# A new head for a diffusion-plus-convolution kernel: negated coefficients, adding DMAs, both divergences on TensorE, another order on every engine

## The reference, cut to what matters

```
s  = groupnorm(x)                                   # 32 groups of 2 channels
g  = relu(bn(dwconv3x3(s, wg)));   g1 = relu(bn(dwconv3x3(s, wg1)))
gy, gx = sobel(s)
Bx = 0.2 / (gy*gy/4 + 1);          By = 0.2 / (gx*gx/4 + 1)
E  = 0.2 * 0.5 * (roll(g,1,W) - roll(g,-1,W) + roll(g1,1,C) - roll(g1,-1,C))   # the divergence
D  = 1 / (1 + 2Bx + 2By);          c0 = 1 - 2Bx - 2By
for 5 steps:                                        # h starts as s, h0 as s
    h, h0 = D*(c0*h0 - 2E*h + (-Ax+2Bx)*roll(h,1,W) + (Ax+2Bx)*roll(h,-1,W)
                 + (-Ay+2By)*roll(h,1,C) + (Ay+2By)*roll(h,-1,C)) + 0.4*D*s,  h
x  = x + relu(bn(h));   x = x + relu(conv3x3(groupnorm(x), ternary(W)) + b)
```

## Time and profile before

| what | us |
|---|---|
| median of 3 runs | 327.84 |
| the profiled execution | 327.07 |
| its span | 324.1 |
| VectorE busy | 270.0 (83%) |
| TensorE busy | 254.3 (78%) |
| ScalarE busy | 129.1 (40%) |
| GpSimd busy | 7.2 (2%) |

### The profile page before, as it was taken

How to read it: one execution, slowest core, us unless ns; L and a number is a source line. 1 busy time by engine, 2 the same in 40 slices (tenths; PEclk the granted TensorE clock), 3 DMA queues, 4 the chain that set the end, 5 groups by cost and what they waited for, 6 DMA issues and landing times.

```text
span 324.1 us, 5181 instructions
## 1 busy us (share of the span) xinstructions
PE 254.3 (78%) x2252; PEld 228.0 (70%) x2252; DVE 270.0 (83%) x224; ACT 129.1 (40%) x198; POOL 7.2 (2%) x25
## 2 busy tenths in 40 slices
PE   0125779999887999997008999999999987788794
PEld 0114569797776996686008999998998977776683
DVE  1896343499899999579999999999999999997921
ACT  3235569905671252512002244152351150451943
POOL 1000000000000000001000001011010000000000
PEclk9999986557995589999656999999999999799999
DMA  7540000000000000000600003361951003000033
GB/s 255 167 157 0 0 0 5 1 2 2 0 2 2 2 2 0 0 2 0 129 0 2 0 2 65 67 129 18 231 111 35 1 0 131 0 2 0 0 129 129
DMA packets 5173, 14.44 MB, mean 45 GB/s; under 512 B 2336, under 2 KB 2336, under 8 KB 4128
## 3 DMA queue, kind: packets, MB, share of 16 engines
q0 software_dynamic: 720, 5.24, 8.0%
q1 hardware_dynamic: 4144, 8.16, 7.7%
q10 hardware_dynamic: 288, 0.72, 0.7%
HBM read 6.79 MB, written 2.10 MB: 27 GB/s over the span
## 4 chain that ended last, share of the span: by engine, by line
DVE 34%; PE 12%; issue 3%; ACT 1%; DVEq 0%; ACTq 0%
DVE ring L796 21%; PE psum L1048 5%; PE psum L1121 4%; DVE first_two L872 3%; DVE stats L809 2%; PE psum L956 2%; DVE coef L839 2%; DVE coef L804 1%; DVE coef L755 1%; DVE coef L771 1%; DVE first_two L576 1%; DVE coef L850 1%; ACT coef L325 0%; DVE lo L845 0%; DVE mv L812 0%
## 5 line engine op out<-in xcount | busy, mean ns | idle before, releaser
L796 DVE TENSOR_TENSOR ring<-coef,state 128x2048 f32<-128x2048 f32 x51 | 113.5, 2290 | 6.2 <-ACT state L325 5.1
L1048 PE MATMUL psum<-mats,ring 128*128 128x128 f32 x816 | 96.0, 277 | 7.0 <-DVE ring L796 6.9
L1048 PEld LDWEIGHTS psum<-mats,ring 128*128 128x128 f32 x816 | 90.9, 143 | 10.6 <-DVE ring L796 10.2
L325 ACT ACTIVATE state<-psum 128x1024 f32<-128x1024 f32 x36 | 35.1, 1024 | 94.2 <-PE psum L1048 60.0
L1007 PEld LDWEIGHTS psum<-coef,state 32*128 32x128 f32 x768 | 36.1, 289 | 2.0 <-issue 2.0
L1007 PE MATMUL psum<-coef,state 32*128 32x64 f32 x768 | 36.8, 378 | 0.0
L1048 PE MATMUL psum<-mats,first_two 128*128 128x128 f32 x144 | 20.7, 306 | 18.6 <-DVE first_two L576 18.6
L576 DVE SCALAR_TENSOR_TENSOR coef<-coef 128x2048 f32<-128x2048 f32 x15 | 34.4, 2291 | 0.4
L1048 PEld LDWEIGHTS psum<-mats,first_two 128*128 128x128 f32 x144 | 19.0, 161 | 18.9 <-issue 18.8
L325 ACT ACTIVATE coef<-psum 128x512 f32<-128x512 f32 (+1 forms) x22 | 17.2, 792 | 33.6 <-PE psum L1007 21.4
L985 PE MATMUL psum<-hi_s,sobel_m 128*128 128x512 f32 (+2 forms) x48 | 21.1, 443 | 7.0 <-DVE lo_s L638 5.8
(11 more groups left out here) (123 smaller groups left out, 265.1 us busy)
## 6 DMA issues: line engine op xcount, KB each, us to landing
first_two<-coef POOLq DMA_DIRECT2D x5, 1024.0 KB, 7.1
coef<-in_x SPq DMA_DIRECT2D x2, 1024.0 KB, 5.8
coef<-in_wide_taps SPq DMA_DIRECT2D x4, 384.0 KB, 4.2
ring<-in_x SPq DMA_DIRECT2D x2, 512.0 KB, 6.4
ring<-in_x SPq DMA_DIRECT2D x1, 1024.0 KB, 9.0
out<-coef SPq DMA_DIRECT2D x2, 512.0 KB, 3.1
out<-coef SPq DMA_DIRECT2D x4, 256.0 KB, 2.5
mats<-in_matrices ACTq DMA_DIRECT2D x1, 384.0 KB, 6.1
```

The costliest lines, as they stand in the source:

```text
L325: return nc.scalar.activation(dst, src, func, **kw)
L796: V.tensor_tensor(wc(ring[:, slot, :]), wc(coef[:, t, a, :]), h_at(t, k, dw, dc), ALU.mult)\
L1048: ins = mm(slot_ap(name)[:, (j % 8) * 128:(j % 8) * 128 + 128], src[:, j * 128:j * 128 + 128], ident, is_transpose=True, start=first and j ...
```

## The change

All of it is in the head. The steps keep their products, in another order.

1. The coefficients are made negated (ScalarE negates when it takes a sum out, `keep_turned`), which lets one scalar-tensor-tensor do what took two operations. `over_rows` and `over_channels` are two operations each and make `AXP` and 2gD in `AXM` (`AYP`, `AYM` likewise); a DMA issued by GpSimd then adds `AXP` to `AXM`. `scaled_g`, `plus_columns`, `minus_columns` and one operation of `over_channels` are gone.
2. Tile 0's divergence goes to TensorE too (`dv_0_0`, `dv_0_1`); both tiles' divergences stand ahead of the first step.
3. The reordered copy is made on VectorE from the centred tile and the inverse root (`scale_grouped`) rather than by ScalarE from the scaled one. `split_hi(1)` moves from ScalarE to VectorE, `shifted` of tile 0 stays there.
4. Centring, squaring and summing the squares go by halves.
5. The taps lie in planes 6 and 5 of tile 1 and in a buffer of their own, so planes 3 and 4 are free; their transfers are issued before and just behind the second tile's `x`. The ternary weights lie in ring buffer 2.
6. In the Sobel jobs all the matmuls on the high part come first. The order of the jobs, of their slots and of the work on every engine is another one.
7. All the second tile's diffusivities come before step (0,0), and its remaining coefficients between steps (0,0) and (1,0) rather than behind (1,0).

```diff
-A0, AE, FS, AXM, AXP, AYM, AYP = 1, 3, 0, 6, 4, 2, 5
+A0, AE, FS, AXM, AXP, AYM, AYP = 1, 6, 0, 3, 4, 2, 5
...
-        taps_m = coef[:, 1, 3:5, :].rearrange("p a n -> p (a n)")[:, 0:CG * 6 * W]\
-            .rearrange("p (g y v n) -> p g y v n", g=CG, y=3, v=2)
+        taps_at = [coef[:, 1, 6, 18 * C:18 * C + 4 * 6 * W], coef[:, 1, 5, 0:10 * 6 * W], last_taps[:, :]]
...
-        wtern = coef[:, 1, 6, 18 * C:27 * C]
+        wtern = ring[:, 2, 0:9 * C]
...                                                    # GpSimd, ahead of its other DMAs
+            for t in range(TILES):
+                pool.wait_ge(axp_ready, t + 1)
+                pool.dma_start(coef[:, t, AXM, :], coef[:, t, AXP, :], accum_op=ALU.add).then_inc(ax_full[t], 16)
+                pool.wait_ge(ayp_ready, t + 1)
+                pool.dma_start(coef[:, t, AYM, :], coef[:, t, AYP, :], accum_op=ALU.add).then_inc(ay_full[t], 16)
...                                                    # ScalarE
-                frees(copy(turned(t, k + 1, h), slot_ap(name)), name)
+                frees(copy(turned(t, k + 1, h), slot_ap(name), scale=-1.0), name)
...                                                    # VectorE
+            def scale_grouped(t):
+                dve.wait_ge(xm_ready, 2 * t + 2)
+                rs = gsum[:, t, 3, :].rearrange("p (a g) -> p a g", a=CP).unsqueeze(3).unsqueeze(4)
+                V.tensor_tensor(s_grouped[t].rearrange("p (g e a w) -> p a g e w", e=2, a=CP, w=W),
+                                h_at(t, 0).rearrange("p w (a g e) -> p a g e w", a=CP, e=2),
+                                rs.broadcast_to([128, CP, CG // 2, 2, W]), ALU.mult).then_inc(s_grouped_ready, 1)
...
+            def over_rows(t):
+                taken_out(t)
+                dve.wait_ge(d_ready, 2 * t + 1)
+                then(stt(coef[:, t, AXM, :], gN[t], 2.0, coef[:, t, 0, :], ALU.mult, ALU.mult))
+                stt(coef[:, t, AXP, :], coef[:, t, AXM, :], -0.5, coef[:, t, AXP, :], ALU.mult, ALU.add)\
+                    .then_inc(axp_ready, 1)
...
-                for i, (a, dw, dc) in enumerate(((AYM, 0, -1), (AYP, 0, 1), (AXM, -1, 0), (AXP, 1, 0), (AE, 0, 0))):
+                for i, (a, dw, dc) in enumerate(((AYP, 0, 1), (AXP, 1, 0), (AE, 0, 0), (AXM, -1, 0), (AYM, 0, -1))):
...
             denominator(0)
-            ternary()
             split_lo(1)
             newton(0)
-            diffusivities(0)
...                                                    # TensorE
+            to_depthwise(0, 0)
+            to_depthwise(0, 1)
+            pe.wait_ge(sobel_m_ready, 4)
+            for g in range(2):
+                for h in range(2):
+                    sobel(0, g, h)
+            group_var(1)
+            depthwise(0, 0)
+            depthwise(0, 1)
...
+            depthwise(1, 0)
+            divergence(0, 0)
+            divergence(0, 1)
+            depthwise(1, 1)
+            divergence(1, 0)
+            divergence(1, 1)
```

More of the change, by code:

```diff
@@ L334, in square_of @@
             def square_of(t):
-                act.wait_ge(xm_ready, t + 1)
-                copy(wc(square), h_at(t, 0), ACT.Square).then_inc(sq_ready, 1)
+                if t:
+                    act.wait_ge(vsum_ready, 2)
+                for h in range(2):
+                    act.wait_ge(xm_ready, 2 * t + h + 1)
+                    copy(wc(half(square, h)), h_at(t, 0, w0=h * W // 2, w1=(h + 1) * W // 2), ACT.Square)\
+                        .then_inc(sq_ready, 1)
             def wrap(t, k, done):
@@ L524, in _ @@
                 keep_turned(k, t, 1)
-                if (k, t) == ORDER[0]:
-                    d_of(1)
                 keep_state(k, t, 0)
@@ L677, in ternary @@
                 wait_reader(dve, "wsum")
-                then(V.tensor_scalar(wred[:, 2:3], wred[:, 1:2], -1.0, None, ALU.mult))
+                V.tensor_scalar(wred[:, 2:3], wred[:, 1:2], -1.0, None, ALU.mult)
+            threshold()
+            scale_s(0)
+            split_hi(0)
+            split_lo(0)
+            centre(1)
+            sum_squares(1)
+            def ternary():
+                dve.wait_ge(vsum_ready, 4)
                 then(V.tensor_scalar(wtern, wabs, wred[:, 1:2], None, ALU.is_gt))
@@ L684, in ternary, with shifted @@
                 signal(stt(wtern, wl, wred[:, 1:2], wabs, ALU.is_ge, ALU.subtract), tern_ready, 1)
+            def shifted(t):
+                for h in range(2):
+                    wait_reader(dve, f"gx_{t}_{h}")
+                V.tensor_scalar(coef[:, t, 2, :], coef[:, t, 1, :], (1.0 + 2 * DT) * S, None, ALU.add)\
+                    .then_inc(shifted_ready, 1)
             def denominator(t):
@@ L709, in newton @@
-                then(stt(c[3], c[3], -2.0, y_first[t], ALU.add, ALU.mult))
-            def diffusivities(t):
-                c = [coef[:, t, i, :] for i in range(NCOEF)]
-                then(stt(c[4], c[1], S, c[3], ALU.add, ALU.mult))
-                then(stt(c[5], c[0], S, c[3], ALU.add, ALU.mult))
-                signal(V.tensor_tensor(c[2], c[4], c[5], ALU.add), sb_ready, t + 1)
-            def divergence(t):
+                then(stt(coef[:, t, 5, :], coef[:, t, 0, :], S, coef[:, t, 3, :], ALU.add, ALU.mult))
@@ L741, in divergence_taken, with source @@
+            def source(t):
                 for h in range(2):
                     wait_reader(dve, f"dv_{t}_{h}")
[L744 to L751 removed]
@@ L866, in step @@
                     dve.wait_ge(halo_ready, 4 * states_through(k - 1, t))
-                for i, (a, dw, dc) in enumerate(((AYM, 0, -1), (AYP, 0, 1), (AXM, -1, 0), (AXP, 1, 0), (AE, 0, 0))):
+                for i, (a, dw, dc) in enumerate(((AYP, 0, 1), (AXP, 1, 0), (AE, 0, 0), (AXM, -1, 0), (AYM, 0, -1))):
+                    if k == 0 and i == 0:
+                        dve.wait_ge(ayp_ready, t + 1)
+                        dve.wait_ge(axp_ready, t + 1)
+                        for h in range(2):
+                            wait_reader(dve, f"dv_{t}_{h}")
+                    if k == 0 and a == AXM:
+                        dve.wait_ge(ax_full[t], 16)
+                    if k == 0 and a == AYM:
+                        dve.wait_ge(ay_full[t], 16)
                     multiply(t, k, a, dw, dc)
@@ L873, in step @@
                         .then_inc(kept_made[t], 1)
+            ternary()
+            ask_scale(1)
+            shifted(0)
+            rsqrt(128, GROUPS, gsum[:, 1, 3, :])
             denominator(0)
-            ternary()
+            scale_grouped(1)
+            scale_s(1)
+            split_hi(1)
             split_lo(1)
             newton(0)
-            diffusivities(0)
+            across_columns(0)
+            across_rows(0)
+            both_diffusivities(0)
             wait_job(dve, "alpha")
@@ L1153, in _ @@
             small("wsum", 1, ones[:, :], wred[:, 0:1])
+            to_depthwise(0, 0)
+            to_depthwise(0, 1)
+            pe.wait_ge(sobel_m_ready, 4)
+            for g in range(2):
+                for h in range(2):
+                    sobel(0, g, h)
+            group_var(1)
+            depthwise(0, 0)
             depthwise(0, 1)
-            pe.wait_ge(kept_ready, 1)
-            small("alpha", 2, ones[:, :], wred[:, 3:5])
+            to_depthwise(1, 0)
+            to_depthwise(1, 1)
             for g in range(2):
@@ L1159, in _ @@
                     sobel(1, g, h)
-            to_depthwise(1, 0)
-            to_depthwise(1, 1)
+            pe.wait_ge(kept_ready, 1)
+            small("alpha", 2, ones[:, :], wred[:, 3:5])
             depthwise(1, 0)
+            divergence(0, 0)
+            divergence(0, 1)
             depthwise(1, 1)
+            divergence(1, 0)
+            divergence(1, 1)
             last = None
             for k, t in ORDER:
-                if last == ORDER[0]:
-                    divergence(1, 0)
-                    back_to_natural(*last)
-                    divergence(1, 1)
-                    add_source(t, k)
-                elif last and last[0] < STEPS - 1 and last[1] != t:
+                if last and last[0] < STEPS - 1 and last[1] != t:
                     add_source(t, k)
```

291 lines of the change are left out of this document (130 added, 161 removed), and 7 rows, old and new, of the table early.

## The result

The kernel before took 328.15 us (median of four runs, 327.47 to 328.92), the changed one 305.78 (304.44 to 307.02): ratio 0.932 [0.927, 0.936], 22 us faster. All four runs before lie in the upper of two groups of times that this kernel has, 321 to 324 and 326 to 329 us; against the lower one the gain is some 17 us (the experiments come to this). The forecast was 317 with a range of 310 to 323, so it was wrong: the change brought twice what I gave it. The profiled execution took 307.02, its span 305.2 (before 327.07 and 324.1).

The account below looks back on a forecast made before the run. VectorE was taken to carry most of the chain, with only the head changing: 10.2 us less work, idle 26.2 against 27.3, step (0,1) 10.5 earlier; 327.07 - 10.5 = 316.6, said as 317 for the median, range 310 to 323.

Parts of the forecast that it names:

- The failed step: TensorE's chain in the head: the clock falls during tile 0's depthwise halves, which take 8.6 and 12.6 us.
- The first rival: Clock stays up through tile 0's depthwise convolutions: 11.1 us less on TensorE's chain, gain 21.6, time 306; chance 0.13.
- The window and what follows it: Head from 21.64 to step (0,1), 151.6 us before, now ending at 162.7; the rest unchanged at 150.9 us.
- Work on VectorE: VectorE's work from 21.64 to step (0,1): 114.3 us by counting operations, 10.2 less than before.
- the grouped scaling: VectorE's plane reading single fp32 elements 264 bytes apart: taken as 2.29 us, bounds 2.2 and 4.6.
- the second rival: The regrouping plane on VectorE costs twice, making the chain 2.3 us longer: 319.5 us; chance 0.15.
- Idle time: VectorE's waits between 21.64 and step (0,1): 26.2 us in sum, against 27.3 before.
- Adding DMAs: Accumulating transfers for AXM and AYM: land after 7.1 us, needed 25 to 35 us after issue, so cost nothing.
- The range: 310 to 323 us: below, half of the first rival; above, the second rival with some 3.5 us of further waits.

Follow-up runs that it names:

- the gap put back: The changed kernel with TensorE's first depthwise half of tile 0 waiting for all 32 scaled taps instead of 16: 322.74 us, ratio 1.001 to the kernel before.
- its filled version: The kernel before with only ScalarE's tap scaling earlier in two places, to fill gaps ahead of tile 0's depthwise halves: 319.52 us, ratio 0.992.

## Why the prediction was wrong

The failed step is "a depthwise half right behind dense work keeps 2.4 GHz for 3.7 to 8.7 us, and the one behind it runs at 1.2 GHz". It turned into an endurance of the depthwise work, counted from the last dense work, and left out what stood between them: the first half that fell had a gap of 2.17 ahead of it, the one that held (90.91) one of 0.61. The longer time, 8.7 us, was counted to a fall at 98.0, and that lies in an idle gap too (96.5 to 99.05). Behind no gap the halves ran 13.1 us at the high clock. The forecast gave TensorE 21.2 us for the two halves and 4.9 for the transposes; they took 13.1 (40.7 to 53.8) and 2.2 (to 56.0). That is 10.8 less; the parts around it gave 1.2 back, which leaves 9.6 on the chain: the first product's sum ended at 119.1, not 128.7. The first rival said just this (first ring buffer free at 117.6, step (0,1) at 151.6, 306), and I gave it 0.13. That its time fits to a fraction of a us is partly luck: the ring buffer came free 1.5 later (119.1) than it says, and it counts 4.0 for transposes that take 2.

Of the 2.7 at the transposes some 2 are a second slip, which no clock explains: the forecast counted a tile's transposes as twice sixteen records. A tile has sixteen, 1.97 at 2.4 GHz (53.82).

By the other steps:

- *The window and what follows it.* Step (0,1) at 152.8, not 162.7. From there on 152.4, against 151: right but for the clock in the closing convolution, which falls in some executions of either kernel.
- *Work on VectorE.* Forecast 114.3, measured 116.8; the grouped scaling, 3.99 instead of 2.29, twice is 3.4 of it, the rest of the count came out 0.9 too high.
- *The grouped scaling* was mis-sized: I took the nearest row on the same engine (L839 in the earlier trace rows, 16 bytes apart) and not ScalarE's twofold for the same pattern. And L839 was read against the wrong row: it has one input, 0.744 for 512 elements, and was set beside a two-input operation, where plain one-input operations of the same trace take 0.52 for 576 and 1.23 for 2048 elements. Beside these it is about one and a half times as long, so it leaned to the second rival too. Singles 264 bytes apart cost 1.74 times a plain plane. The Trainium skill ("Advanced Engine Details and Errata", SBUF Cachelines) says that an access which finds a different line each time is penalised (it names no engine). The trace agrees, for VectorE with 3.99 against 2.29. The second rival came true, but in time it was small, 2 to 3 us lost beside 20 gained.
- *Idle time.* Forecast 26.2, measured 14.5. The waits of 9.2 for alpha and 1.8 for the shifted copy hung on the clock and are not there; tile 0's divergence waits 3.28 (forecast 4.7), the fourth product 7.63 (7.4), the inverse root 2.26 (2.5), var_1 1.03 (0.6). With the gap put back, the two that are missing came, as 8.03 and 2.40.
- *Adding DMAs.* They land in 7.3 us (the forecast's 7.1) and are waited for nowhere, as forecast; the kept sums' land in 8.1 instead of 7.1, which nothing waits for either.
- *The range* took in half of the first rival. Since a clock step decides between two outcomes and both were in the trace, it should have reached to that rival's end, 306.

## What to carry to other kernels

Before you say that a kind of matmul can't hold the clock, read in the same rows the gap in front of it: work like these depthwise halves kept a clock that it never brought back, and then the one wait ahead of it sets the price of all that comes behind. Let the engine that feeds TensorE run ahead of such work; where it can't, a few transposes in the gap may do it (they did in the one gap where they were tried, ahead of matmuls of 512 columns; ahead of a depthwise half it is untested). Look also at how the unchanged kernel's times lie: two groups were a sign that its clock met both outcomes. Moving work from a full engine to another brings no time where the full one then waits for the other: look whose wait ends last (here VectorE gave away 7 us of divergence, and the time stayed).

## What the runs showed of the hardware

- Behind these gaps a depthwise half (192 records on 32 rows) kept 2.4 GHz: none, and 0.61 (six profiles). Behind these it ran at 1.2 GHz: with another depthwise half ahead of the gap 1.05, 2.40 to 2.56 (ahead of depthwise (1,1) in all six profiles of the kernel before and its filled version), 3.59 and 8.07; with Sobel matmuls ahead 3.84. At 1.72 two of four executions had the low mean clock and at 2.17 four of five profiles, with the same code. What decides there, and whether the depthwise half ahead of the gap matters, is not shown by these runs.
- A depthwise half at 1.2 GHz stayed so to its end in every profile (10.52 us instead of 5.59); the clock came back in other work only: in the changed kernel the six records at 98.23 take 3.50, the eight behind them 2.25 as at the high clock (87.14); with the gap put back the sixteen transposes at 69.64 take 2.95 and the Sobel matmuls behind them run at full rate (seven in 1.73).
- VectorE, two fp32 inputs of 2048 elements: 2.29 us contiguous, 3.99 when it reads singles 264 bytes apart, 3.63 and 3.77 when it writes them 512 bytes apart.
